# Two decoder layers on one core: the work that prepares a block, put into the block of the norm ahead of it

## What is computed

```python
def _layernorm(x, axis=-1, eps=1e-05):
    m = jnp.mean(x, axis=axis, keepdims=True)
    v = jnp.var(x, axis=axis, keepdims=True)
    return (x - m) / jnp.sqrt(v + eps)
```

## Time and profile before

| | |
|---|---|
| median of 3 runs | 3224.19 us (3223.34 to 3226.42) |
| the profiled execution | 3216.19 us, its span 3214.4 us |
| busy: PE, DVE, ACT, POOL | 2543.4, 1876.0, 1638.4, 886.7 us |
| mean granted TensorE clock | 0.857 of full speed |
| DMA | 192.65 MB, mean 60 GB/s |

### The profile page before, as it was taken

How to read it: one execution, slowest core, us unless ns; L and a number is a source line. 1 busy time by engine, 2 the same in 40 slices (tenths; PEclk the granted TensorE clock), 3 DMA queues, 4 the chain that set the end, 5 groups by cost and what they waited for, 6 DMA issues and landing times. The chain is left out here.

```text
span 3214.4 us, 45471 instructions
## 1 busy us (share of the span) xinstructions
PE 2543.4 (79%) x12893; PEld 1583.9 (49%) x12895; DVE 1876.0 (58%) x3887; ACT 1638.4 (51%) x3615; POOL 886.7 (28%) x746
## 2 busy tenths in 40 slices
PE   4799999889999984777769558877478658789894
PEld 2466666546666653444435323333344323555552
DVE  4688888668888875888851367773322432233334
ACT  2577777557777752888941126555155300223331
POOL 1344444334444440000000200000100047344443
PEclk8999999989999986666669759898688867999997
DMA  1121122012122105700000000000000043678875
GB/s 63 53 60 34 53 60 40 7 41 59 40 60 60 38 2 178 243 1 1 1 32 0 18 1 1 1 1 1 23 1 0 1 145 124 140 165 179 176 166 127
DMA packets 127068, 192.65 MB, mean 60 GB/s; under 512 B 17552, under 2 KB 88208, under 8 KB 125584
## 3 DMA queue, kind: packets, MB, share of 16 engines
q1 hardware_dynamic: 83696, 134.71, 14.8%
q0 software_dynamic: 23616, 33.24, 5.8%
q10 hardware_dynamic: 19584, 22.57, 2.5%
HBM read 123.23 MB, written 67.25 MB: 59 GB/s over the span
## 5 line engine op out<-in xcount | busy, mean ns | idle before, releaser
L234 DVE SCALAR_TENSOR_TENSOR h_pre<-h_px,h_par,h_pre 128x510 f32<-128x510 f32 (+2 forms) x384 | 286.3, 746 | 132.9 <-ACT h_pre L675 112.8
L568 POOL TENSOR_TENSOR h_mix<-h_decay,cb 128x768 f32<-128x768 f32 x128 | 235.0, 1836 | 421.6 <-ACT h_decay L656 421.6
L2861 POOL DMA_INDIRECT moe_sums<-ex_y,ex_sidx x132 | 205.5, 1557 | 241.9 <-DVE ex_y L3040 218.0
L600 PE MATMUL h_px<-x_cols,h_w 128*128 128x512 f32 x512 | 246.7, 605 | 21.6 <-DMA h_d<-d_skip 21.6
L605 PE MATMUL h_pz<-x_cols,h_w 128*128 128x512 f32 x512 | 243.5, 598 | 10.0 <-DVE h_gate L714 9.9
L635 PE MATMUL h_po<-h_wo,h_h 128*128 128x256 f32 x1024 | 241.8, 380 | 3.2 <-issue 3.2
L687 ACT ACTIVATE h_xt<-h_pxt,h_sel 128x128 f32<-128x128 f32 x512 | 145.9, 368 | 147.1 <-PE h_pxt L624 147.1
L2913 PE MATMUL ex_pg<-ex_w,ex_xT 128*128 x528 | 195.2, 493 | 20.3 <-ACT ex_xT L2969 6.2
L1224 ACT ACTIVATE xq_ex<-xq_ps,xq_nmax,xq_qs 128x512 f32<-128x512 f32 x256 | 205.4, 847 | 2.4 <-DVE xq_nmax L1280 2.4
L635 PEld LDWEIGHTS h_po<-h_wo,h_h 128*128 128x128 f32 x1024 | 185.4, 191 | 23.2 <-issue 3.6
L820 POOL TENSOR_TENSOR norm_rstd<-norm_mv,mhalf 128x4 f32<-128x4 f32 x24 | 28.2, 1176 | 605.5 <-DVE norm_mv L803 605.5
(11 more groups left out here) (390 smaller groups left out, 5760.1 us busy)
## 6 DMA issues: line engine op xcount, KB each, us to landing
h_cumb<-cum_rows SPq DMA_DIRECT2D x32, 1024.0 KB, 8.3
moe_tiles<-blank SPq DMA_DIRECT2D x4, 6642.0 KB, 44.6
ex_w<-moe_w SPq DMA_DIRECT2D x64, 352.0 KB
ex_xg<-moe_tiles ACTq DMA_DIRECT2D x136, 162.0 KB, 2.7
ex_wd<-moe_wd SPq DMA_DIRECT2D x64, 176.0 KB
h_w<-w_xg SPq DMA_DIRECT2D x8, 1024.0 KB, 11.1
moe_sums<-blank SPq DMA_DIRECT2D x2, 2176.0 KB, 26.7
h_wo<-w_out SPq DMA_DIRECT2D x8, 512.0 KB, 10.9
```

The source lines that it names most:

```text
L234: ins = dve.scalar_tensor_tensor(out=out[:, :, back:S], in0=src[:, :, 0:S - back], scalar=par[:, at + CK - 1 - back:at + CK - back], in1=o ...
L568: pool.tensor_tensor(mix[j % 2][:], decay[j][:], cbj, ALU.mult).then_inc(matched, 1)
L600: mm = pe.matmul(px[j % 2][:].rearrange("p u l -> p (u l)"), w_in[s.pg][:, k, j, 0, :], r.xT[:, k, s.p * 2 * S:(s.p + 1) * 2 * S], start=( ...
L2861: pool.indirect_dma_start(out=r.sums[i % 2][:, :], out_offset=bass.IndirectOffsetOnAxis(ap=sidx[i][:, 0:1], axis=0), in_=y[i % 2][:], in_o ...
```

## The change

`norm_stage` takes a second set of instruction lists, `Beside`, and puts each into its own block: on SP the loads; on GpSimd `pool` ahead of the four roots; on TensorE `first` ahead of the norm's transposes and `tensor` behind them; on ScalarE and VectorE behind the norm's own work. The norm's number of PSUM pairs becomes a parameter (`bufs`). The norms between the sublayers are now called by the stage that follows them. The first context passes its projection as `first`, and its transposes go into the banks of xc_pk and xc_pv instead of four banks of their own, so xc_vb is now made ahead of the key split. The feed forward passes its loads and the scaling of fa_wd. The quantised weights pass everything. The second context passes the key half of its projection as `first`, the rest as `tensor`, with `bufs=1`. The semaphores of these parts live for the whole program, so the clearing block behind the first context is gone.

```diff
+        self.ahead = {name: ctx.enter_context(nc.semaphore(name)) for name in
+                      ("xc_loaded", "xc_multiplied", "xc_split", "xc_turned", "xc_freed", "f0_loaded", "f0_scaled",
...
-def norm_stage(nc, a, r, index, out=None):
+class Beside:
+    def __init__(self, sync=None, first=None, tensor=None, scalar=None, vector=None, pool=None):
...
+def norm_stage(nc, a, r, index, out=None, beside=Beside(), bufs=2):
...
-        pt = [[ctx.enter_context(nc.psum_tensor(f"{tag}_pt{i}{k}", [P, U * P], F32)) for k in range(KE)] for i in range(2)]
+        pt = [[ctx.enter_context(nc.psum_tensor(f"{tag}_pt{i}{k}", [P, U * P], F32)) for k in range(KE)] for i in range(bufs)]
...
                 ins.then_inc(normed, 1)
+            if beside.vector:
+                beside.vector(dve)
...
             forget(pool, r)
+            if beside.pool:
+                beside.pool(pool)
             for t in range(TURNS):
...
+        if beside.sync:
+            @block.sync
+            def _(sp):
+                beside.sync(sp)
...
         @block.tensor
         def _(pe):
+            if beside.first:
+                beside.first(pe)
             for t in range(TURNS):
                 pe.wait_ge(normed, at + t + 1)
-                pe.wait_ge(kept, LEAD + at + t - 1)
+                pe.wait_ge(kept, LEAD + at + t + 1 - bufs)
...
                 mm.then_inc(turned, 1)
+            if beside.tensor:
+                beside.tensor(pe)
...
                 ins.then_inc(kept, 1)
+            if beside.scalar:
+                beside.scalar(act)
...
-        xattn0_context(nc, a, r, keysT, vals, wq, wp, bq, bp)
+        with ExitStack() as held:
+            norm_stage(nc, a, r, 0, beside=xattn0_context(nc, a, r, held, keysT, vals, wq, wp, bq, bp))
...
-        pt = [psum(f"pt{i}", [P, 8 * P], BF16) for i in range(4)]
+    pt = [one[:].rearrange("p a e -> p (a e)").bitcast(BF16) for one in pk] + [one[:].bitcast(BF16) for one in pv]
...
+    return Beside(sync=sync, first=tensor, tensor=transposes, vector=vector)
...
+        norm_stage(nc, a, r, 1, beside=Beside(sync=sync, vector=vector))
...
-        attn1_weights(nc, a, r, wqkv, wout, wscale)
+        with ExitStack() as held:
+            norm_stage(nc, a, r, 2, beside=attn1_weights(nc, a, r, held, wqkv, wout, wscale))
...
-        xattn1_context(nc, a, r, keysT, vals, wq)
+        with ExitStack() as held:
+            norm_stage(nc, a, r, 3, beside=xattn1_context(nc, a, r, held, keysT, vals, wq), bufs=1)
...
+    return Beside(sync=sync, first=first, tensor=tensor, scalar=scalar, vector=vector, pool=gpsimd)
...
+        norm_stage(nc, a, r, 4)
         aug = sb("aug", [P, NT, ROW])
...
-        for n, stage in enumerate((mamba_stage, xattn0_stage, ffn0_stage, attn1_stage, xattn1_stage, moe_stage)):
+        for stage in (mamba_stage, xattn0_stage, ffn0_stage, attn1_stage, xattn1_stage, moe_stage):
             stage(nc, a, r)
-            norm_stage(nc, a, r, n, out if n == 5 else None)
+        norm_stage(nc, a, r, 5, out)
```

More of the change, by code:

```diff
@@ L998, in _ @@
[L998 to L1005 removed]
+            if part < 2:
+                dve.tensor_tensor(resh, resh, parts[:, :, part * XD:(part + 1) * XD], ALU.subtract)
@@ new lines, in vector @@
+        dve.nop().then_inc(split, 1)
+        dve.tensor_reduce(vs[:], vb[:], AX.X, ALU.max, apply_absolute_value=True)
+        dve.drain()
+        fake_quant_scales(dve, vs[:], vr[:], vs[:], 1.0 / 127, 1.0)
+        for f in range(KE):
+            dve.tensor_scalar(vb[:, f, :], vb[:, f, :], vr[:, f:f + 1], ROUND, ALU.mult, ALU.add)
+            dve.tensor_scalar(wp[:, f, :], wp[:, f, :], vs[:, f:f + 1], None, ALU.mult)
+        dve.drain()
+        dve.tensor_scalar(vi[:], vb[:], ROUND, None, ALU.subtract).then_inc(split, 1)
@@ L1359, in ffn0_stage @@
         hid = sb("hid", [P, FT, C])
-        pg = [psum(f"pg{i}", [P, C]) for i in range(2)]
-        pu = [psum(f"pu{i}", [P, C]) for i in range(2)]
-        po = [psum(f"po{i}", [P, 512]) for i in range(2)]
-        loaded = sem("loaded")
-        scaled = sem("scaled")
+        loaded, scaled = r.ahead["f0_loaded"], r.ahead["f0_scaled"]
         gated = sem("gated")
@@ L1378, in _, with vector @@
             sp.dma_start(dscl[:], a["f0_sd"].partition_broadcast(P)).then_inc(loaded, 16)
+        def vector(dve):
+            dve.wait_ge(loaded, 80)
+            dve.tensor_tensor(wd[:], wd[:], dscl[:, None, :].to_broadcast([P, FT, E]), ALU.mult).then_inc(scaled, 1)
+        norm_stage(nc, a, r, 1, beside=Beside(sync=sync, vector=vector))
+        pg = [psum(f"pg{i}", [P, C]) for i in range(2)]
+        pu = [psum(f"pu{i}", [P, C]) for i in range(2)]
+        po = [psum(f"po{i}", [P, 512]) for i in range(2)]
+        block = ctx.enter_context(nc.Block())
         @block.tensor
@@ new lines, in attn1_weights, with sb, sem, sync @@
+def attn1_weights(nc, a, r, ctx, wqkv, wout, wscale):
+    def sb(name, shape, dt=F32):
+        return ctx.enter_context(nc.sbuf_tensor("aw_" + name, shape, dt))
+    def sem(name):
+        return r.ahead["aw_" + name]
+    raw = [sb("qkv", [P, KE, AQKV]), sb("out", [P, KE, E])]
+    sums = sb("sums", [P, 2])
+    inv = sb("inv", [P, 2])
+    ps = ctx.enter_context(nc.psum_tensor("aw_ps", [P, 512], F32))
+    loaded = sem("loaded")
+    summed = sem("summed")
+    spread = sem("spread")
+    def sync(sp):
+        for dst, name in zip(raw, ("a1_wqkv", "a1_wout")):
+            sp.dma_start(dst[:], a[name].rearrange("(k p) f -> p k f", p=P)).then_inc(loaded, 16)
+    def tensor(pe):
+        pe.wait_ge(summed, 1)
+        pe.matmul(ps[:, 0:2], r.ones[:], sums[:], start=True, stop=True).then_inc(spread, 1)
+    def vector(dve):
+        dve.wait_ge(loaded, 32)
+        for n, w in enumerate(raw):
+            ins = dve.tensor_reduce(sums[:, n:n + 1], w[:], AX.XY, ALU.add, apply_absolute_value=True)
+        ins.then_inc(summed, 1)
+        dve.wait_ge(spread, 1)
+        for n, w in enumerate(raw):
+            dve.tensor_scalar(wscale[:, n:n + 1], ps[:, n:n + 1], 1.0 / (w.shape[1] * w.shape[2] * P), BIT_EPS,
+                              ALU.mult, ALU.max)
+        dve.drain()
+        dve.reciprocal(inv[:], wscale[:])
+        dve.drain()
+        for n, (w, q) in enumerate(zip(raw, (wqkv, wout))):
+            dve.tensor_scalar(w[:], w[:], inv[:, n:n + 1], ROUND, ALU.mult, ALU.add)
```

434 lines of the change are left out of this document (187 added, 247 removed).

## The result

| | before | changed |
|---|---|---|
| median of the runs | 3223.77 us (4 runs, 3219.78 to 3226.42) | 3170.11 us (4 runs, 3165.34 to 3173.74) |
| profiled execution, its span | 3216.19, 3214.4 us | 3171.19, 3169.4 us |
| mean granted clock | 0.857 | 0.869 |

From one profiled execution to the other the span fell by 45.0.

What follows compares the result with a forecast made beforehand. No engine is busy throughout; norms and following blocks' fronts stand one behind the other across barriers. Gains 17.8 + 9.0 + 7.1 + 8.7 = 42.6 us, from median 3224.19, give 3181.6 us; range 3173 to 3190.

Steps and rivals of the forecast that it cites:

- First context: First norm to first queries: loads and projection run beside the norm, gaining 17.8 us, bounds 17.0 and 18.2.
- the spare time ahead of the key chain: First context: VectorE finishes norm and fill 2.9 us before TensorE's projection lets the key chain start.
- the hidden transposes: First context: norm's transposes end before the key transposes are asked for; those, 3.44 us, stay covered by 0.5 us.
- Feed forward: Second norm to first matmul: loads hidden whole behind the norm, gaining 9.0 us, bounds 8.5 and 11.
- the clock's bound: Feed forward's start: beginning at the upper clock level would give back 1.95 us; none was counted in the forecast.
- Quantised weights: Third norm to tokens block: loads hidden, VectorE delayed by TensorE's last norm transposes; gain 7.1 us, between 6.6 and 7.6.
- Second context: Fourth norm and second context: loads and key half of projection beside the norm, gaining 8.7 us, bounds 6.7 and 11.8.
- the halves' distance: Second context: starts of the projection's two halves lie 18.3 us apart, where before they lay 11.22 apart.
- The turns: Second context: four norm transpose turns between the projection's halves, two at either clock level, 9.9 us together.
- The rule that I weighed: Second context: short idles between PSUM-cycling bursts drop the clock repeatedly, so no turn counts on the upper level; gain 6.7 us.
- Better clock: Rival: fast turns in the second context and a fast feed forward start, gain 48.2 us, 3176.0; chance 0.11.
- the slower rival: Rival: attention over tokens' clock falls; mean 0.71 eats the whole gain, 0.65 gives 3257 us; chance 0.03.

Runs made afterwards that it cites:

- the reference: Unchanged kernel before, timed beside each subject of a comparison; 3225.82 us (19 runs) beside its first copy.
- the three copies of one program: The kernel before, unchanged, timed as subject against itself: 3219.25, 3222.68 and 3217.97 us.
- the run of the feed forward's part: Against the kernel before, only the feed forward's loads and scaling beside the second norm, other pieces behind their norms in own blocks: 3208.01 us, ratio 0.9944.
- the two versions that load earlier: Changed kernel with both contexts' projection operands loaded a block ahead; fills behind GpSimd's roots: 3165.79 us, ratio 0.9811; fills on ScalarE: 3152.93 us, ratio 0.9787.
- the third execution: Third profiled execution of the unchanged kernel before; its comparison gave 3222.68 us (12 runs), ratio 0.9999.
- The repeat: The changed kernel, unchanged, as a second profiled execution and five more runs beside the kernel before: 3173.00 us, ratio 0.9842.

## Why the prediction was wrong

**The step that failed** is "its time lay 8.0 below the median 3224.19, so for the median of runs I say 3181.6", and in the range "the 3 us by which runs differ". Both were taken from three runs within 3.1 us. The first profiled execution was not fast by a fixed 8 us that the changed kernel's would also be: the changed kernel's was 1.1 slower than the median of its runs, and its three profiled executions took 3171.19, 3177.03 and 3169.05 against a mean of its 13 runs of 3172.75. As the subject of a comparison the kernel before had 36 runs from 3210.67 to 3227.39, with a mean of 3220.06, and its four profiled executions took 3216.19, 3214.78, 3224.03 and 3220.43. The miss of 11.5 us is these 8.0, the 2.4 by which the forecast for the profiled execution, 3173.6, missed the measured 3171.19, and the 1.1 by which that lay above the median.

Of the 53.7 us between the first medians some 46 are borne out. Copy against copy in one session, the means lie 45.7 us (12 and 5 runs) and 45.8 us (24 and 4 runs) apart, and the means of the profiled spans 46.4. Against the reference of the same sessions it is 51.0 and 47.6, as that came out 5.3 and 1.8 us above the copies beside it. Over all sessions 47.3 us remain between the means of 36 and 13 runs (ratio 0.9853), and 50.3 if the reference runs are counted too (107 runs, mean 3223.08). Whether a reference comes out higher than a subject for a reason stays open: the three copies of one program gave 0.9985, 0.9999 and 0.9987.

Point by point:
- **First context**, 17.8 forecast, 16.7 measured, under its lower bound of 17.0. From the first load to the first matmul it took 10.46, 10.89 and 9.88 us beside the norm where 9.2 was forecast, and the projection 9.51, 9.21 and 9.89 for 8.93. Both forecasts came from one execution, with the shortest projection of four: the other three had 9.56, 9.86 and 9.20 for the load and 9.39, 9.23 and 9.68 for the projection. In means the load is 0.95 us longer beside the norm and the projection 0.23; that the norm is what makes the load longer is not shown, for with the same loads behind the norm, in the run of the feed forward's part, it took 10.47. The order on VectorE, the spare time ahead of the key chain and the hidden transposes were right.
- **Feed forward**, 9.0 forecast, 8.9 measured to the first matmul. But the clock's bound went only one way. The windows of its start and its rest in the changed kernel, with those of attention over tokens and the four turns (columns as above):

```profile
1647.29:1653.30 6.01, 6.01 (x7) 2.51 (x8) 0.00 (x0) 0.00 (x0) 0.00 (x0) 0.50 0.01 3
1653.30:1783.20 129.90, 122.13 (x378) 71.09 (x376) 24.79 (x40) 21.63 (x28) 0.00 (x0) 1.00 0.00 0
1803.30:2221.40 418.10, 299.96 (x2560) 137.24 (x2560) 256.06 (x576) 210.85 (x273) 42.87 (x95) 0.82 0.01 3
2238.89:2248.10 9.21, 5.41 (x33) 4.62 (x32) 7.58 (x9) 3.26 (x6) 0.00 (x0) 0.77 0.00 0
```

  The lower level lasts 6.0 us here and 4.0 in the kernel before, and the stage is 1.1 longer in the three profiles of the changed kernel and in that of this part alone: 2.0 more us at half speed are worth 1.0. Net 7.9, below the 8.5 I had called the bound. The idle time ahead does not decide it: in the two versions that load earlier TensorE stands idle for the same 1.89 us behind the same transposes, the lower level lasts 3.4 us, and the stage takes 134.6:

```profile
1645.22:1648.62 3.40, 3.40 (x4) 1.51 (x5) 0.00 (x0) 0.00 (x0) 0.00 (x0) 0.50 0.02 5
1648.62:1651.23 2.61, 2.61 (x7) 1.14 (x6) 0.00 (x0) 0.53 (x1) 0.00 (x0) 1.00 0.00 0
```

  What sets its length I did not find.
- **Quantised weights**, 7.1 forecast, 7.4 measured; TensorE's last transposes were the delay, as worked out.
- **Second context**, 8.7 forecast, 11.8 measured between means, at its upper bound. 9.8 came from the first pair of profiles, where the load's lead, the halves' distance (17.9 us for 18.3) and the second half (1.1 longer for 1.4) each came out some 0.3 to 0.6 better than forecast; 2 from my base, whose 61.86 was the shortest of four: its two halves of the projection took 8.56 and 7.17 us, those of the third execution 10.02 and 8.82. The turns were right in kind (a fast pair first) but the share of slow ones is a matter of the execution. The repeat, which had all four fast, in windows over the turns and the second half:

```profile
2245.70:2253.50 7.80, 4.00 (x33) 3.38 (x32) 7.33 (x8) 3.26 (x6) 0.00 (x0) 1.00 0.00 0
2253.56:2260.60 7.04, 7.04 (x34) 5.89 (x32) 0.23 (x1) 2.68 (x4) 0.00 (x0) 1.00 0.00 0
```

  With TensorE busy for 4.00 of 7.80 us the clock stayed at 1.00. In the first profile it stood at 0.77 over the same four turns (last of the windows above). The rule that I weighed (the Trainium skill, "TensorE: Matmul & The Clock Gate", "A second HAM failure mode: psum-queue depth-cycling") gives 6.7 by my sum; no execution came near it, though the third had one slow turn and the first one and a half. (That sum has a slip: four slow turns are 3 x 3.23 + 1.97 = 11.7 us, not 11.4, and the bound is then 6.4.) GpSimd's fills ahead of the roots, for which I allowed VectorE 0.5, cost nothing: the norm ran 2221.40 to 2234.84, 13.44 us.
- **The rivals.** Better clock (3176.0) came nearest and had the right sign, but for the second context alone; the feed forward went the other way. Attention over tokens, where the slower rival would have decided, ran at 0.82 for 0.81.

With the extra 1.1 of the feed forward the four terms sum to 43.7, one more than forecast. That it comes so near is partly luck: 3.1 too little for the second context stands against 1.1 too much each for the first context and the feed forward. The mechanism held; the base and the spread did not.

## What to carry

Take a base for a sum from several executions, or state the forecast as a difference; the scatter of the program is measured by its runs, and three that agree don't measure it. Work that is put beside a norm is worth its length only once its operands have landed: the next step, loading them a block ahead with the fills on ScalarE, took another 17.8 us off the two contexts' stretches, more than the parts of the feed forward and the weights together (16.3). And look at what shares a path with the engine that is busiest there before a fill is handed to an idle one.

## What the runs showed of the hardware

One scaling on VectorE of 0.41 us took 3.53 while GpSimd filled a tile for 3.61; the statistics beside the changed kernel's fills did not grow (1.41 us) while a four-column TENSOR_SCALAR took 0.60, ending 0.02 from the fill's end, and 0.17 elsewhere, in a fill of ScalarE's too. The Trainium skill ("SBUF — State Buffer", "Who interferes with whom") calls it an exclusive lock on a pair of ports that VectorE and GpSimd share, which tensor_scalar can take and which the later of the two waits for whole: the trace agrees, and ScalarE, which filled for as long (3.62), held nobody up. The feed forward's matmuls began at a granted clock of 0.50 for 4.0 us in the kernel before, 6.0 in the changed one and 3.4 in the versions that load a block ahead, with hardly a difference between executions of one program. Attention over tokens came in two lengths round 418 and 424 us in one program, with TensorE busy for 298.56 and 304.35; what decides between them I did not find.
